# Attention scores of batches 1 to 15 by seven block products instead of eight, in a fused attention and gated feed-forward kernel

## What is computed

```python
x = L0_attn_t                                   # (16, 1024, 256) fp32
qkv = layernorm(x) @ W_qkv.T + b_qkv            # Q, K, V of width 256
attn = softmax(Q @ K.T / 16)
x = x + layernorm(attn @ V)
y = layernorm(x)
h = silu(y @ (w_gate/127).T) * (y @ (w_up/127).T)   # 768 wide
out = x + layernorm(h @ (w_down/127).T)
```

## Time and profile before

| | us |
|---|---|
| median of three runs | 1382.4 |
| lowest and highest | 1381.77, 1383.32 |
| the profiled execution | 1381.28 |
| its span, first to last instruction | 1379.5 |
| TensorE busy | 1347.5 |
| VectorE busy | 897.7 |
| ScalarE busy | 879.5 |
| GpSimd busy | 826.1 |

### The profile page before, as it was taken

One profiled execution on the slowest core, in us unless ns is written; L12 is line 12 of the kernel. 1 busy time (PEld: TensorE's weight loads), 2 busy tenths in 40 slices (PEclk: granted clock), 3 DMA queues, 4 the chain that ended last, 5 costly groups with the idle time before them and its releaser, 6 DMA issues.

```text
span 1379.5 us, 22219 instructions
## 1 busy us (share of the span) xinstructions
PE 1347.5 (98%) x7332; PEld 721.1 (52%) x7332; DVE 897.7 (65%) x2160; ACT 879.5 (64%) x1373; POOL 826.1 (60%) x1002
## 2 busy tenths in 40 slices
PE   6898999999999999999999999999999999999987
PEld 3353555554555545555554555545555555555544
DVE  5875666666657667666666656667566666657565
ACT  4757575675766567575775757567575774756544
POOL 1768376484746748376484755748376484745544
PEclk9999999999999999999999999999999999999999
DMA  6997382653827457383653736547373664716311
GB/s 191 175 186 166 55 160 68 138 133 69 161 77 130 115 96 141 88 154 73 134 142 69 161 78 122 123 92 146 79 151 85 121 135 82 136 56 121 92 36 51
DMA packets 437175, 158.27 MB, mean 115 GB/s; under 512 B 418113, under 2 KB 420417, under 8 KB 437058
## 3 DMA queue, kind: packets, MB, share of 16 engines
q1 hardware_dynamic: 436272, 156.03, 54.5%
q10 hardware_dynamic: 786, 0.79, 0.2%
HBM read 36.70 MB, written 16.78 MB: 39 GB/s over the span
## 4 chain that ended last, share of the span: by engine, by line
PE 94%; DVE 3%; issue 1%; DMA 1%; POOL 1%; ACT 0%; ACTq 0%; POOLq 0%
PE S L710 93%; DMA hTh<-in_L_attn_W_qkv 1%; DVE mxs L613 0%; DVE S L642 0%; DVE st L651 0%; POOL rs L293 0%; PE S L736 0%; DMA yTl<-yl 0%; DVE st L669 0%; DVE X L664 0%; DVE hf L679 0%; DVE zw L606 0%; POOL yl L365 0%; DVE xl L320 0%; ACT yn L458 0%
## 5 line engine op out<-in xcount | busy, mean ns | idle before, releaser
L438 ACT ACTIVATE P<-S,nmx,sc 128x1024 f32<-128x1024 f32 x128 | 154.0, 1203 | 282.5 <-DVE nmx L617 282.5
L613 DVE TENSOR_REDUCE mxs<-S 128x1 f32<-128x1024 f32 x128 | 156.2, 1220 | 125.0 <-PE S L710 124.7
L679 DVE SCALAR_TENSOR_TENSOR hf<-S,sc,hf 128x512 f32<-128x512 f32 x192 | 142.0, 746 | 140.1 <-ACT hf L473 134.3
L338 POOL TENSOR_TENSOR Pl<-P,Ph 128x1024 f16<-128x1024 f32 x96 | 206.0, 2147 | 33.9 <-issue 26.4
L710 PE MATMUL S<-xTh,zTh 128*128 128x512 f16 x512 | 194.6, 380 | 4.4 <-ACT P L438 2.2
L710 PE MATMUL S<-PTh,xh 128*128 128x512 f16 x512 | 194.0, 379 | 1.0 <-DVE hf L679 1.0
L710 PE MATMUL S<-xTh,zTl 128*128 128x512 f16 x512 | 194.8, 380 | 0.0
L710 PE MATMUL S<-xTl,zTh 128*128 128x512 f16 x512 | 194.7, 380 | 0.0
L710 PE MATMUL S<-PTl,xh 128*128 128x512 f16 x512 | 194.0, 379 | 0.0
L710 PE MATMUL S<-PTh,xl 128*128 128x512 f16 x512 | 194.0, 379 | 0.0
L289 POOL TENSOR_SCALAR rs<-mv,sc 128x2 f32<-128x2 f32 (+1 forms) x96 | 35.3, 368 | 230.7 <-DVE mv L655 191.3
(11 more groups left out here) (113 smaller groups left out, 2462.2 us busy)
## 6 DMA issues: line engine op xcount, KB each, us to landing
xs<-in_L_attn_t SPq DMA_DIRECT2D x32, 512.0 KB, 5.3
X<-in_L_attn_t SPq DMA_DIRECT2D x32, 512.0 KB, 4.6
out_x<-X SPq DMA_DIRECT2D x64, 256.0 KB, 2.9
PTh<-Ph SPq DMA_TRANSPOSE x128, 3.2
PTl<-Pl SPq DMA_TRANSPOSE x128, 3.3
hTh<-in_L_attn_W_qkv ACTq DMA_DIRECT2D x1, 768.0 KB, 7.2
hTl<-in_L_ffn_w_gate SPq DMA_DIRECT2D x1, 768.0 KB, 7.2
hTh<-in_L_ffn_w_up SPq DMA_DIRECT2D x1, 768.0 KB, 9.0
```

The lines of the kernel that those rows point to most:

```text
L338: p.engine.tensor_tensor(out=Pl[:, m % 3, :], in0=P[:, m % 2, :], in1=Ph[:, m % 3, :], op=ALU.subtract).then_inc(pl_vector if i in PL_ON_V ...
L438: a.engine.activation(P[:, m % 2, :], ps[:, bank:bank + 2, :].rearrange("p a n -> p (a n)"), ACT.Exp, bias=nmx[:, c:c + 1], scale=sS, accu ...
L613: v.engine.tensor_reduce(mxs[:, c:c + 1], ps[:, bank:bank + 2, :].rearrange("p a n -> p (a n)"), axis=AX.X, op=ALU.max, negate=True).then_ ...
L679: v.engine.scalar_tensor_tensor(out=hf[:, n % 3, :], in0=ps[:, bank + 1, :], scalar=sc2[:, 4:5], in1=hf[:, n % 3, :], op0=ALU.mult, op1=AL ...
```

## The change

The scores of a pair of query blocks (2j, 2j + 1) by all keys form a 2 by 2 block product with an inner dimension of 2 times 128. Eight products of blocks (each three fp16 matmuls of 512 columns) become seven, by Strassen's method in Winograd's form. So `score` stays for batch 0 alone, and for the other batches `score_first` (products P1, P6, P2, P5, P7) and `score_second` (P3, P4) take its place, one of each for j = 0 to 3.

The sums of blocks that the seven products need are made on the other engines: `x_mix` (VectorE, four of 128x512 a batch) makes four differences of xhat in place, which `T_high`, `T_low` and four more DMA transposes `turn_T` split and turn. `z_mix` (VectorE, eight of 128x256 a batch), `zm_high` (ScalarE) and `zm_low` (GpSimd) do that for z. `z_high` writes its tiles in three parts of 128x256 for each half instead of two of 128x512.

The results are put together in PSUM and on VectorE. P1 lands in bank 1, ScalarE copies it to SBUF (`copy_P1`), then P5 adds to bank 1, which is copied again (`copy_P15`), then P3 adds to it. P6 lands in bank 2, is copied (`copy_P6`), then P7 adds, then P4. Four `join` instructions per j (VectorE, `tensor_tensor_reduce`, 128x512, with a running maximum) make the four blocks of scores and the row maxima, in place of two `row_max`.

```diff
+        def score_first(t, b, j, free0, free1, free2, free3):
...
+            t.wait_ge(*free1)
+            product(t, 1, j, 0, x_block(b, 0, 0), True).then_inc(P1_done, 1)
+            t.wait_ge(*free2)
+            product(t, 2, j, 5, T_block(1, 1), True).then_inc(P6_done, 1)
+            t.wait_ge(*free0)
+            product(t, 0, j, 1, x_block(b, 0, 1), True).then_inc(P2_done, 1)
+            t.wait_ge(s1_done, n + 1)
+            product(t, 1, j, 4, T_block(0, 0), False).then_inc(P5_done, 1)
+            t.wait_ge(s6_done, n + 1)
+            t.wait_ge(*free3)
+            product(t, 2, j, 3, T_block(1, 0), False).then_inc(P7_done, 1)
+
+        def score_second(t, b, j):
+            n = 4 * (b - 1) + j
+            t.wait_ge(s15_done, n + 1)
+            product(t, 1, j, 6, x_block(b, 1, 1), False).then_inc(P3_done, 1)
+            t.wait_ge(C22_done, n + 1)
+            product(t, 2, j, 2, T_block(0, 1), False).then_inc(P4_done, 1)
```

```diff
+        def copy_P15(a, b, j):
+            n = 4 * (b - 1) + j
+            a.wait_ge(P5_done, n + 1)
+            a.wait_ge(C22_done, n)
+            a.engine.activation(s15[:, :], ps[:, 1, :], ACT.Copy).then_inc(s15_done, 1)
...
+        def add_max(v, out, a, s, seed, top):
+            return v.engine.tensor_tensor_reduce(out=out, in0=a, in1=s, scale=1.0, scalar=seed, op0=ALU.add, op1=ALU.max,
+                                                 accum_out=top)
...
+        def join_C22(v, b, j):
+            n = 4 * (b - 1) + j
+            v.wait_ge(P7_done, n + 1)
+            v.wait_ge(s15_done, n + 1)
+            add_max(v, ps[:, 3, :], ps[:, 2, :], s15[:, :], LOWEST, mxs[:, n % 2, 2:3]).then_inc(C22_done, 1)
+
+        def join_C12(v, b, j):
+            n = 4 * (b - 1) + j
+            v.wait_ge(P3_done, n + 1)
+            v.wait_ge(s6_done, n + 1)
+            v.wait_ge(C11_done, n + 1)
+            add_max(v, ps[:, 1, :], ps[:, 1, :], s6[:, :], mxs[:, n % 2, 0:1], mxs[:, n % 2, 1:2]).then_inc(C12_done, 1)
+            v.wait_ge(C12_done, n + 1)
+            nmx_of(v, 8 * b + 2 * j, mxs[:, n % 2, 1:2])
```

The lists of all five queues are written anew. TensorE, one period (scores of b + 1; what follows stands in the order of before except where shown):

```diff
+                attend(t, b, 0, 0, (silu_done, 12 * b - 1))
+                attend(t, b, 0, 1)
+                score_first(t, b + 1, 1, (exp_done, 8 * b + 9), (exp_done, 8 * b + 9), (exp_done, 8 * b + 10), (exp_done, 8 * b + 10))
+                project_v(t, b, 0, (ft_done[0], 4 * b - 2), (ft_done[1], 4 * b - 2))
+                attend(t, b, 1, 2, (ol_done[1], 2 * b + 1))
+                score_second(t, b + 1, 1)
+                attend(t, b, 1, 0, (ol_done[0], 2 * b + 1))
+                attend(t, b, 1, 3)
+                score_first(t, b + 1, 2, (exp_done, 8 * b + 11), (exp_done, 8 * b + 11), (exp_done, 8 * b + 12), (exp_done, 8 * b + 12))
+                score_second(t, b + 1, 2)
                 attend(t, b, 1, 1)
+                score_first(t, b + 1, 3, (exp_done, 8 * b + 13), (exp_done, 8 * b + 13), (exp_done, 8 * b + 14), (exp_done, 8 * b + 14))
                 project_v(t, b, 1, (x1_done, 8 * b + 2), (x1_done, 8 * b + 4))
+                score_second(t, b + 1, 3)
                 gate_up(t, b, 0, 0, 6, (ol_done[0], 2 * b + 2), (ol_done[1], 2 * b + 2), three)
...
                 down(t, b, 0, 0, (ft_done[0], 4 * b), three)
+                attend(t, b + 1, 0, 2, (hmul_done, 12 * b + 11))
+                score_first(t, b + 2, 0, (silu_done, 12 * b + 12), (hmul_done, 12 * b + 12), (silu_done, 12 * b + 10), (hmul_done, 12 * b + 10))
+                attend(t, b + 1, 0, 3)
+                score_second(t, b + 2, 0)
                 down(t, b, 0, 1, (ft_done[1], 4 * b), three)
```

Between `gate_up(b, 0, 0)` and the first `gate_up` of the second half there now stand five gates, two `down` of b - 1 and the two `project_z`. The stretch of VectorE's list that goes with j = 2 and 3, and the one of ScalarE's:

```diff
+                join_C11(v, b + 2, 2)
+                join_C22(v, b + 2, 2)
+                join_C12(v, b + 2, 2)
+                join_C21(v, b + 2, 2)
+                o_low(v, b + 1, 1, 0)
+                join_C11(v, b + 2, 3)
+                p_low(v, b + 2, 4)
+                y_scale(v, b + 1, 1, 0)
+                y_stats(v, b + 1, 1, 0)
+                join_C22(v, b + 2, 3)
+                join_C12(v, b + 2, 3)
+                join_C21(v, b + 2, 3)
+                y_scale(v, b + 1, 1, 1)
+                y_stats(v, b + 1, 1, 1)
+                x_mix(v, b + 3, 0)
```

```diff
+                exp(a, b - 1, 3, 2)
+                o_high(a, b - 2, 1, 1)
+                copy_P1(a, b - 1, 2)
+                p_high(a, b - 1, 3)
+                copy_P6(a, b - 1, 2)
+                copy_P15(a, b - 1, 2)
...
+                copy_P1(a, b - 1, 3)
+                copy_P6(a, b - 1, 3)
+                y_high(a, b - 2, 0)
+                p_high(a, b - 1, 4)
+                p_high(a, b - 1, 5)
+                copy_P15(a, b - 1, 3)
```

GpSimd's list has, between the two `x1_norm` and the last gate of a period, `y_low(b, 1)` behind `h_low(b, 0, 0)`, `h_low(b, 0, 1)` and a `d_norm`, and then `z_low`, `T_low(1)`, `T_low(0)`, `zm_low(0)`, `z_low`, `zm_low(1)` among the `h_low`. At the end all gates of batch 14 stand ahead of the value products of 15:

```diff
+            project_v(t, 15, 0, (ft_done[0], 58), (ft_done[1], 58))
+            attend(t, 15, 1, 2, (ol_done[1], 31))
             attend(t, 15, 1, 0, (ol_done[0], 31))
+            attend(t, 15, 1, 3)
             attend(t, 15, 1, 1)
             project_v(t, 15, 1, (x1_done, 122), (x1_done, 124))
             gate_up(t, 15, 0, 0, 6, (ol_done[0], 32), (ol_done[1], 32), three)
...
             gate_up(t, 15, 1, 5, 2, (silu_done, 189), (hmul_done, 189), three)
+            down(t, 15, 0, 0, (ft_done[0], 60), three)
+            down(t, 15, 0, 1, (ft_done[1], 60), three)
+            down(t, 15, 1, 0, (ft_done[0], 62), three)
             down(t, 15, 1, 1, (ft_done[1], 62), three)
```

More of the change, by code:

```diff
@@ L1119, in _ @@
+                z_low(p, b + 3, 0)
+                h_low(p, b + 1, 0, 3)
+                d_norm(p, b, 1, 1)
+                h_low(p, b + 1, 0, 4)
+                p_low(p, b + 2, 7)
+                T_low(p, b + 3, 1)
+                h_low(p, b + 1, 1, 0)
+                h_low(p, b + 1, 1, 1)
+                T_low(p, b + 3, 0)
+                zm_low(p, b + 3, 0)
+                z_low(p, b + 3, 1)
+                d_norm(p, b + 1, 0, 0)
+                zm_low(p, b + 3, 1)
             h_low(p, 13, 1, 3)
@@ L1330, in _ @@
+            x_hat(a, 15, 1, 0)
+            x_hat(a, 15, 1, 1)
             exp(a, 14, 2, 0)
@@ L1387, in _ @@
+            copy_P15(a, 15, 0)
+            o_high(a, 14, 0, 1)
+            exp(a, 15, 0, 0)
+            exp(a, 15, 1, 2)
+            p_high(a, 15, 0)
+            p_high(a, 15, 1)
+            add_bias(a, 13, 0, 1)
+            o_high(a, 14, 0, 0)
+            copy_P1(a, 15, 1)
+            copy_P6(a, 15, 1)
+            copy_P15(a, 15, 1)
             exp(a, 15, 2, 0)
             p_high(a, 15, 2)
-            add_bias(a, 13, 1, 0)
             exp(a, 15, 3, 2)
+            o_high(a, 14, 1, 1)
@@ L1420, in _ @@
[L1420 to L1433 removed]
+            h_high(a, 14, 0, 5)
@@ L1874, in second_part @@
-            attend(t, 14, 0, 3)
-            down(t, 13, 1, 0, (ft_done[0], 54), three)
             attend(t, 14, 0, 1)
-            score(t, 15, 0, 0, (silu_done, 168), (hmul_done, 168))
-            score(t, 15, 1, 2, (silu_done, 166), (hmul_done, 166))
+            score_first(t, 15, 1, (exp_done, 121), (exp_done, 121), (exp_done, 122), (exp_done, 122))
+            project_v(t, 14, 0, (ft_done[0], 54), (ft_done[1], 54))
+            attend(t, 14, 1, 2, (ol_done[1], 29))
+            score_second(t, 15, 1)
```

1603 lines of the change are left out of this document (883 added, 720 removed).

## The result

The changed kernel takes **1459.3 us** (median of 4 runs, 1456.6 to 1460.5) against 1382.1 us (4 runs, 1381.4 to 1383.3): a ratio of 1.0555, 95% interval 1.0541 to 1.0569. I had predicted 1397 us, 1378 to 1424: slower is right, and the size is five times too small, +77 instead of +15. One execution of all those in this document, the third of E2, was slow (1477.6 us at a granted clock of 0.93), and E2's time is the median of the other three.

A forecast was written before the change was run, and what follows sets the result against it. TensorE was taken as the bound, never waiting inside a period. To the profiled 1381.3 us it added 3.2 (waits less saving), 8.2 (end) and 3.0 (start): 1395.7, plus 1.1 for the median, say 1397 us; range 1378 to 1424.

The forecast's parts named there:

- The saving: TensorE does 24 matmuls per j and batch as 21, 180 fewer in 15 batches, all on the path: 38.8 us less.
- (a): At j = 3, P4 waits for `join_C22`, which stands behind `y_scale` and `y_stats` on VectorE: 2.07 us in every batch.
- (b): At j = 2, P7 waits 0.3 us for ScalarE's `copy_P6` and P4 0.4 us for join C22: 0.7 us a batch.
- rival of slow joins: VectorE's joins with a running maximum take 1.5 us each, 1.3 us more a batch: 1416 us; chance 0.16.
- For j = 0 and 1 ... I find no wait: At j = 0 and 1, one or two groups of 2.59 us of TensorE work lie between the products: no wait.
- These loads I cost at nothing where they are not on a chain: Work added on ScalarE, VectorE and GpSimd, each about 65 of 80 us, is covered by TensorE's own work: 0 us.
- GpSimd and VectorE in each other's way: Rival: two-source VectorE instructions contend with GpSimd, mostly in the gates; TensorE waits about 1 us a batch: 1411 us; chance 0.16.
- The three small edits: The ring of three `X`, the scratch size and `x_hat` in halves, covered by an early reload: no cost.
- The end: In the last batches, two waits for `yTl` of about 6 us, each followed by slow matmuls: 8.2 us more in sum.
- The start: Three weight loads delay the attention weights, 2 us, and batch 0's first copies and sums cost 1 us: 3 us more.
- "crowded" exps: At the start, the first copies and sums stand among the crowded exps of batch 0: 1 us more, between 0 and 4.

The follow-up runs named there:

- E2: The changed kernel with ScalarE's `copy_P1` and `copy_P6` of j = 0 ahead of `zm_high` of half 1, batches 3 to 15: 1445.1 us.
- E1: The changed kernel with VectorE's `join_C22` of j = 3 moved ahead of `y_scale` and `y_stats` of half 1: 1458.8 us.
- E11: The kernel before plus side work on scratch that nothing waits for, batches 1 to 12: twelve two-source subtractions on VectorE, five subtractions on GpSimd: 1419.6 us.
- E12: As E11, but VectorE's twelve subtractions replaced by one-source statistics of the same input lengths: 1401.4 us.
- E3: The changed kernel with the twelve `x_mix` and `z_mix` instructions per batch replaced by one-source scalings by 1.0, so scores differ from the reference: 1440.2 us.

## Why the prediction was wrong

**The saving**: 7152 matmuls, 38.8 us; the ledger closes with it.

**Waits (a) and (b)**, 42.0 us predicted over 15 batches. Measured: the joins 41.6 and `copy_P6` 5.1, 46.7 in all. (a) is 2.24 beyond the pitch against 2.07; (b) 0.34 and 0.37 against 0.3 and 0.4. A join is 0.84 to 0.90 against 0.85, which settles the rival of slow joins: it did not come. But E1 shows that (a) was no term that could be undone alone.

**"For j = 0 and 1 ... I find no wait"** failed for j = 0: 1.17 us in 13 batches, 14.8 us. I looked at what TensorE has between the products and not at what stands ahead of `copy_P1` on ScalarE: `zm_high`, `z_mix` and `zm_low`, over three engines. E2 shows it (14.1 us back).

**"These loads I cost at nothing where they are not on a chain"** is the step that failed most. The rest of the periods, 88.1 - 38.4 = 49.7 us, is `copy_P1` (14.8), `hf` (12.1), `x1_add` (5.8), `z_float` (3.0), `yTl` and others, and the half clock behind the waits (9.8). I compared sums, 65 of 80 us, and VectorE in fact came to 70 of 86. A sum says nothing of an in-order list in which `h_mul`, `z_float` and the joins must each come within a us or two. E11 prices it: 37.9 us for the side work alone, before any dependence of the new products. The rival **GpSimd and VectorE in each other's way** had the right mechanism with 1 us a batch (14 us) and a chance of 0.16. It took a hold-up as 0.4 us on GpSimd's side; the row that it read, VectorE's `hTl` of 1.11 us for 0.68, already showed VectorE standing still for the rest of a GpSimd instruction, which in the changed kernel is 1.0 or 1.7 us for nearly every `p_low`. E12 against E11 gives 18 us over 12 batches, 1.5 each, for contention, and as much again for order. Of E11's sum in the changed kernel itself only E2 and E3 speak (14 and 19 us, overlapping at `copy_P1`); how the rest splits is open. The three small edits that the prediction took at nothing were not run alone.

**The end**, +8.2 predicted, +14.7 in the ledger, or +11.8 without the joins in it. The two waits for `yTl` were 5.9 and 4.75 us (6.1 and 6.0 predicted), with the slow matmuls behind:

```profile
1360.66 0.61 PE L854 MATMUL S<-yTh,Gh 128*128 128x512 f16 x1 [5.89 <-DMA yTl<-yl]
...
1412.37 0.51 PE L854 MATMUL S<-yTh,Gh 128*128 128x512 f16 x1 [4.75 <-DMA yTl<-yl]
```

Missed: two waits of 1.5 us for `oTh`, where `project_v` of batch 15 follows straight on the last `attend`.

**The start**, +3 predicted, +14.7 measured, 9.4 without the joins and `copy_P6` in it. The weights land after 8.9 us, 1.7 later (2 predicted). The "crowded" exps had 1 us in the sum: the first exp of batch 0 starts at 41.6 us instead of 32.1.

Put together: 4.7 for the named waits, 49.7 for the others in the periods, 3.6 for the end, 6.4 for the start are 64.4 us; the time missed by 62.
